# A post-norm transformer layer on one core: mask rows filled by two engines, a second store queue, TensorE occupied before the first exponential, feed-forward normalised in place

## What is computed

```python
q = einsum('btc,hcd->bhtd', x, Wq) + bq      # the same for k and v
scores = einsum('bhtd,bhsd->bhts', q, k) * D ** -0.5
probs = softmax(scores + causal, axis=-1)
x = layernorm(x + (einsum('bhts,bhsd->bhtd', probs, v) as [B, T, C]) @ Wo + bo)
gate = silu((x @ fp8(gate_w)) * gate_scale)
fuse = gate * ((x @ fp8(up_w)) * up_scale)
x = layernorm(x + (fuse @ fp8(down_w)) * down_scale)
```

## Time and profile before

| | us |
|---|---|
| median of 3 runs (lowest, highest) | 589.0 (588.6, 592.25) |
| the profiled execution's own time | 590.27 |
| its span, first to last instruction | 588.5 |
| TensorE busy | 539.8 (92%) |
| VectorE busy | 443.7 (75%) |
| ScalarE busy | 325.2 (55%) |
| GpSimd busy | 220.3 (37%) |

### The profile page before, as it was taken

How to read it: one execution, slowest core, us unless ns; L and a number is a source line. 1 busy time by engine, 2 the same in 40 slices (tenths; PEclk the granted TensorE clock), 3 DMA queues, 4 the chain that set the end, 5 groups by cost and what they waited for, 6 DMA issues and landing times.

```text
span 588.5 us, 10775 instructions
## 1 busy us (share of the span) xinstructions
PE 539.8 (92%) x3968; PEld 357.9 (61%) x3968; DVE 443.7 (75%) x802; ACT 325.2 (55%) x578; POOL 220.3 (37%) x250
## 2 busy tenths in 40 slices
PE   4568699999999999999999999987899999999993
PEld 1333356656566556665665656654378888888883
DVE  4476567788788878888878888878545877778765
ACT  1206456666766667667666576664854544345430
POOL 3004332433344333443254334421335553455442
PEclk9858989999999999999999999999999999999998
DMA  6878846547446564744654744520000001110012
GB/s 158 224 220 247 231 125 163 170 138 196 150 111 195 148 164 148 183 149 144 144 184 125 200 146 125 155 51 3 2 1 0 8 31 36 37 37 16 22 36 73
DMA packets 62959, 69.07 MB, mean 117 GB/s; under 512 B 7418, under 2 KB 57210, under 8 KB 62906
## 3 DMA queue, kind: packets, MB, share of 16 engines
q1 hardware_dynamic: 62074, 67.85, 40.2%
q10 hardware_dynamic: 832, 0.53, 0.3%
HBM read 37.63 MB, written 29.62 MB: 114 GB/s over the span
## 4 chain that ended last, share of the span: by engine, by line
PE 79%; DVE 6%; DMA 5%; issue 4%; ACT 3%; SPq 1%; POOL 1%; ACTq 0%; POOLq 0%; DVEq 0%
PE ps L1008 13%; PE ps L893 12%; PE ps L885 12%; PE ps L804 10%; PE ps L812 9%; PE ps L1021 7%; PE ps L869 7%; PE ps L870 4%; DVE nmax L576 2%; DMA q_st<-zero_rows 2%; PE ps L835 2%; PE ps L828 2%; DMA m_scratch<-mrow 2%; PE ps L846 1%; DVE hT_l L641 1%
## 5 line engine op out<-in xcount | busy, mean ns | idle before, releaser
L576 DVE TENSOR_REDUCE nmax<-ps 128x2 f32<-128x1024 f32 (+1 forms) x192 | 196.9, 1041 | 76.3 <-PE ps L870 76.1
L421 ACT ACTIVATE probs<-ps 128x512 f32<-128x512 f32 x320 | 183.3, 594 | 80.8 <-PE ps L885 80.7
L346 POOL TENSOR_SCALAR_AFFINE_SELECT probs<-probs 128x512 f32<-128x512 f32 x128 | 86.6, 690 | 199.4 <-ACT probs L421 199.4
L885 PE MATMUL ps<-q_st,k_st 98*128 98x384 bf16 (+3 forms) x512 | 123.3, 304 | 5.4 <-ACT probs L421 3.2
L869 PE MATMUL ps<-k_st,q_st 98*128 98x256 bf16 (+2 forms) x384 | 85.1, 282 | 14.9 <-DMA q_st<-zero_rows 10.8
L374 POOL TENSOR_TENSOR f_l<-f_full,f_h 128x512 fp32r<-128x512 f32 x48 | 61.6, 1290 | 76.6 <-ACT f_h L494 76.6
L870 PE MATMUL ps<-k_st,q_st 124*128 124x128 bf16 x512 | 86.8, 226 | 0.0
L893 PE MATMUL ps<-probs,v_st 128*32 128x512 f32 (+3 forms) x1024 | 84.1, 447 | 0.2
L885 PEld LDWEIGHTS ps<-q_st,k_st 98*128 98x128 bf16 x512 | 44.1, 98 | 50.7 <-issue 27.1
L489 ACT ACTIVATE sgate<-ps,s_gate 128x512 f32<-128x512 f32 x48 | 32.9, 688 | 63.0 <-PE ps L1008 63.0
L869 PEld LDWEIGHTS ps<-k_st,q_st 98*128 98x128 bf16 x384 | 38.5, 100 | 36.3 <-issue 14.7
(11 more groups left out here) (85 smaller groups left out, 810.5 us busy)
## 6 DMA issues: line engine op xcount, KB each, us to landing
q_st<-q_scratch SPq DMA_DIRECT2D x32, 384.0 KB
k_st<-k_scratch SPq DMA_DIRECT2D x32, 384.0 KB
q_scratch<-part SPq DMA_DIRECT2D x16, 384.0 KB, 3.6
k_scratch<-part SPq DMA_DIRECT2D x16, 384.0 KB, 2.8
xT<-in_attn_xT SPq DMA_DIRECT2D x8, 512.0 KB, 3.9
q_scratch<-part SPq DMA_DIRECT2D x16, 256.0 KB, 3.7
k_scratch<-part SPq DMA_DIRECT2D x16, 256.0 KB, 2.0
resid<-in_attn_x SPq DMA_DIRECT2D x8, 512.0 KB, 3.8
```

The source lines that it names most:

```text
L346: pool.affine_select(out=blocks, in_=blocks, compare_op=ALU.is_ge, fill=0.0, base=0, pattern=[*pattern, [1, P]], channel_multiplier=-1).th ...
L421: act.activation(probs[:, u, :], ps[:, u % 2, :], ACT.Exp, scale=SCALE).then_inc(exp_done, 1)
L576: dve.tensor_reduce(nmax[:, i, heads[0]:heads[-1] + 1], src, AX.X, ALU.max, negate=True).then_inc(max_taken, 1)
L885: m = pe.matmul(ps[:, u % 2, c0:c0 + T - P * j], k_st[0:RP, g, h, P * j:P * j + P], q_st[0:RP, g, h, P * j:T], start=True, stop=True)
```

## The change

- **Mask rows.** The two DMAs that copied the mask patterns are gone. `fill_mask` copies a pattern into the stacks of two groups in one instruction: VectorE for groups 0 and 1, GpSimd for groups 2 and 3, each for queries and keys. The patterns now lie on the partitions of their stack rows. The copies begin at partition `R0` = 96, so they also write stack rows 96 and 97, and `load_stack(0, 0)` waits for VectorE's copies and `load_stack(0, 2)` for GpSimd's.
- **Constants.** The memsets of `v_st` move behind the first parts, the one of `k_st`'s rows 0 and 1 is split between VectorE and GpSimd, and the zero rows of all groups come by one DMA at the start in place of one in each first `load_stack`.
- **Two store queues.** ScalarE issues the stores of the high and middle key parts of groups 0 and 1, and the store and load of the first group's maxima. SyncE issues the biases; `xT` of sequence 1 is loaded before the parts are stored.
- **TensorE occupied.** `keep_warm` issues matmuls on a tile of zeros: 10 before the projections, 4 behind the first V projection, 2 behind nearly each unit of maxima of groups 0 and 1. ScalarE's first activation runs on the same tile. `project_qk(0, 0)` waits for the query weights alone.
- **Feed-forward.** `norm_in` writes into `resid`; it stands before `fuse(n+1, 2)`. `make_hT(n + 2)` stands before `gate_up(n+1, 4)` and no longer behind it. The statistics of the output stand before `fuse(n+1, 4)` and the moments before `fuse(n+1, 5)`; `take_rstd2(n)` stands before `f_lo(n+1, 5)`.
- **Tail.** The last `down` goes by chunks into four banks, and the last output is stored in two halves.

The normalisation has moved ahead of the sums whose first halves (`y_sum<-ps`) release `make_hT`. The diff, cut to its core:

```diff
+        def fill_mask(eng, stack, rows, g):
+            return eng.tensor_copy(stack[R0:RA, g:g + 2].rearrange("p g h (b t) -> p (g h b) t", b=TB),
+                                   rows[R0:RA, :].unsqueeze(1).to_broadcast([RA - R0, 2 * HG * TB, P]))
...
@@ SyncE
+                if n:
+                    sp.dma_start(q_st[0:RM, g], zero_rows[:, :].unsqueeze(1).to_broadcast([RM, HG, T])).then_inc(stack_loaded[g], 16)
...
-            sp.wait_ge(pool_const, CONSTS)
-            for stack, rows in ((q_st, mask_q), (k_st, mask_k)):
-                sp.dma_start(stack[RP:RA].rearrange("p g h (b t) -> p (g h b) t", b=TB),
-                             rows[:, :].unsqueeze(1).to_broadcast([RA - RP, G * HG * TB, P])).then_inc(mask_loaded, 16)
+            load_xT(1)
             store_parts(0, 0)
-            store_parts(0, 1)
-            sp.wait_ge(dve_const, 6)
+            sp.wait_ge(lo_ready[1], 1)
+            sp.dma_start(k_scratch[0:P, 0:3, :], part[:, 1, :, :]).then_inc(part_stored[1], 16)
+            sp.wait_ge(mask_filled, 2)
             load_stack(0, 0)
             load_stack(0, 1)
             store_parts(0, 2)
             store_parts(0, 3)
+            sp.wait_ge(mask_filled_late, 3)
             load_stack(0, 2)
-            load_xT(1)
-            store_mrow(0, 0)
-            load_mrow(0, 0)
...
@@ GpSimd
+            pool.memset(k_st[0:RM, 2:G].rearrange("p g h t -> p (g h t)").bitcast(F32), ONES).then_inc(mask_filled_late, 1)
+            pool.wait_ge(pool_const, CONSTS)
+            for stack, rows in ((q_st, mask_q), (k_st, mask_k)):
+                fill_mask(pool, stack, rows, 2).then_inc(mask_filled_late, 1)
...
@@ ScalarE
+            for m in (0, 1):
+                hi_part(0, m, MX + m)
+            for m in (0, 1):
+                mid_part(0, m, probs[:, m, :])
+            dst = k_scratch[0:P]
+            act.wait_ge(mid_ready[1], 1)
+            act.dma_start(dst[:, 3:5, :], part[:, 1, 0:2, :]).then_inc(part_stored[1], 16)
+            act.dma_start(dst[:, 5:6, :], part[:, 1, 0:1, :]).then_inc(part_stored[1], 16)
...
             empty_mT(0)
+            act.wait_ge(mT_out, 1)
+            act.dma_start(m_scratch[0], mrow[0:RM * HG, :]).then_inc(mrow_stored[0], 16)
+            act.wait_ge(mrow_stored[0], 16)
+            act.dma_start(q_st[0:RM, 0], m_scratch[0].rearrange("(a h) t -> a h t", h=HG)).then_inc(mrow_loaded[0], 16)
...
@@ TensorE
+            def keep_warm(count):
+                for _ in range(count):
+                    pe.matmul(ps[:, 1, :], warm[:, 0:P], warm[:], start=True, stop=True)
...
+            pe.wait_ge(warm_ready, 1)
+            keep_warm(10)
...
             for u in range(NM):
                 scores_max(0, u)
+                if u:
+                    keep_warm(2)
             scores_max(1, 0)
             transpose_max(0)
             for u in range(1, NM):
                 scores_max(1, u)
+                keep_warm(2)
...
                 if nxt:
                     gate_up(n + 1, 1 - par, 3)
+                if nxt2:
+                    make_hT(n + 2)
+                if nxt:
                     gate_up(n + 1, 1 - par, 4)
-                if nxt2:
-                    make_hT(n + 2, par)
-                if nxt:
                     gate_up(n + 1, 1 - par, 5)
```

More of the change, by code:

```diff
@@ L385, in _ @@
             for n in range(B):
-                for ic in range(IC):
-                    if n + 1 < B:
+                if n + 1 < B:
+                    for ic in range(IC - 1):
                         f_lo(n + 1, 1 - n % 2, ic)
                 take_rstd2(n)
+                if n + 1 < B:
+                    f_lo(n + 1, 1 - n % 2, IC - 1)
         @block.scalar
@@ L499, in _ @@
                         empty_ynT(B - 1, 1, MB)
[L500 removed]
+                    if n > 0 and n + 1 < B and ic == 4:
                         for c in range(KC):
@@ L773, in _ @@
                 if nxt:
+                    out_stats(n, 0)
+                    out_stats(n, 1)
+                    fuse(n + 1, 4)
+                    out_moments(n)
                     fuse(n + 1, 5)
-                    out_stats(n, 0)
-                out_stats(n, 1)
-                out_moments(n)
-                if not nxt:
+                else:
+                    out_stats(n, 1)
+                    out_moments(n)
                     norm_out(n)
```

171 lines of the change are left out of this document (103 added, 68 removed).

## The result

| | before | after |
|---|---|---|
| median (lowest, highest), 16 runs each | 589.63 (588.07, 593.65) | 587.47 (586.83, 589.05) |
| span of the profiled execution | 588.5 | 585.1 |
| TensorE's mean granted clock | 0.967 | 0.971 |

The ratio of after to before is 0.9958, with an interval of 0.9942 to 0.9974. The change wins 0.0042 x 589.6 = 2.5 us where 8.3 were predicted, which is less than the 1% that the prediction took as the bound of no change. The interval leaves out 1, so a small gain is real.

A forecast was written before the change was run, and what follows sets the result against it. Bounds: the start's transfers and waits, one feed-forward wait a period, VectorE's tail; mid-attention is TensorE-bound. Terms 0.3 + 0.35 - 2.3 - 2.6 - 3.0 - 0.5 - 0.5 = -8.25 take 589.0 to 580.7 us; forecast within 578.5 to 583, full range 574.0 to 584.5.

The forecast's parts named there:

- the round trip of the maxima: Start, group 0's maxima through DRAM: on ScalarE's queue the trip fits under TensorE's own work, -2.3 us.
- the bound of 0: Round trip of the maxima: the gain is 0 instead of -2.3 us if the store still takes 4.77.
- TensorE's own order: Between transposes and first scores: group 1's maxima units and the last two occupying matmuls need 5.2 us.
- The first exponentials: Dense TensorE work from 42.8 on: 5.2 us at the low clock take half at the high level, -2.6 us.
- Rival 2: Waits only change name: slow round trip, low clock or down_out eats the gain; any one 583.0 to 583.7; chance 0.20.
- The start up to the first stack: From projections to first stack issue: early projections' gain is lost to the port GpSimd and VectorE share, +0.3 us.
- The maxima: Maxima loop of group 0: clock starts low and TensorE leads for three or four units, +0.35 us.
- From there to 73.8 nothing changes: First exponentials to 73.8 us: no change; the wait for the next stack, bound by DMA engines, moves along.
- Feed-forward: Feed-forward periods: earlier transposes remove the hT_l wait but slip 0.2; 0.5 us a period won, -3.0 in all.
- Tail: Last down by chunks: only 8 of 48 matmuls remain behind the last f_lo, now behind GpSimd's rstd; -0.5 us.
- the last store: End of the span: half the bytes in the last output store save about 0.5 of 3.4 us, -0.5.

The follow-up runs named there:

- e7_trip_port: After, with SyncE issuing the first round trip ahead of the bulk loads and GpSimd's memset and mask copies started behind the last low part; 578.4 us (0.9794).
- e14_all_late: After with SyncE's round trip before bulk, GpSimd copies behind low parts, wider act_warm, and up/down weights, output weights and scales loaded later; 568.2 us (0.9630).
- e1_hold_bulk: After, with SyncE waiting until the first group's maxima are back in the stack before issuing load_raw(0), load_x(0) and load_stack(0, 3); 583.4 us (0.9886).
- e3_no_port: After, with GpSimd starting its memset and mask copies only when VectorE has written all four low parts; 584.6 us (0.9901).
- e13_after_weights_late: After, with only the loads of the feed-forward up and down weights moved to the second sequence's turn; 581.3 us (0.9860).
- e6_aligned: After, with act_warm 48 bytes wider so that later SBUF tiles begin at a multiple of 64 bytes again; 585.4 us (0.9912).
- e5_ffn_alone: Before, with only the new feed-forward stage and tail, keeping its own start and SBUF layout; 583.4 us (0.9880).

## Why the prediction was wrong

**The failed step is the round trip of the maxima**: "On ScalarE's own queue I take 2.3, which makes 1.2 + 2.3 + 1.5 = 5.0 and lies under the 5.2." The sum for it was -2.3. Transposes to first scores took 44.60 - 33.76 = 10.84 us, 7.48 before, so the term is +3.4. It has two errors. The store was priced by its queue, from the 1.46 us of a later one that had nothing ahead of it; behind the 768 KB of the third stack it takes 4 to 5 us (e7_trip_port 4.02, e14_all_late 4.17, e2_sync_trip 4.95, all from SyncE), and from ScalarE, behind 2.4 MB, it took 5.37. And the bound of 0 was no bound: the prediction counted what the trip had ahead of it and not what the move released. SyncE's wait for the trip had held back 2 MB; with the wait gone they ran beside it, and the load, 1.48 us before, took 4.37. e1_hold_bulk, which only holds these transfers back, is 4.1 us quicker than after, and e2_sync_trip, which restores the old order on SyncE, 4.9. Even there the trip takes 7.50 us, as before, and e1_hold_bulk, with the trip on ScalarE's queue, is no quicker in total than this kernel. TensorE's own order, taken as 5.2, was 5.6 (7.50 less its wait of 1.91).

**The first exponentials, -2.6, fell with it.** The wait before them was to shrink from 1.75 us to nothing and grew to 5.27, and the clock was at the low level for some 5 of the 5.5 us from 44.60 on, as before. In e2_sync_trip the clock is 1.00 there. From the first scores to the fourth group's maxima it takes 22.59 us there, 24.97 in after and 25.40 before: the mechanism was right and its condition did not hold. Rival 2 ("the waits only change their name") named both effects, but with prices of +2.3 and +2.6, measured from the forecast; the first turned out at 5.7.

**The start up to the first stack** was +0.3 predicted and -1.05 measured, the size alone. The order was the worked one: the first `first_lo` waited for the first copy, the second for the second copy. But all of it came sooner. GpSimd's first copy started at 9.98 and not at 10.5; the copies took 3.59 and 4.06 us (3.9 taken), and the second started without the 0.7 us of `first_lo` between them, so the second `first_lo` ended at 18.12 and not at 19.7. The key store landed after 2.30 us (2.9), and VectorE's copy took 1.22 (1.5). The page weighed there, the Trainium skill, "GPSIMD Engine Reference", section "Performance versus the Vector engine", gives 3.5 by estimate; the copies of 3.59 us in after (the first) and of 3.60 in e3_no_port agree. Nothing was said of the other way out, to start GpSimd later, which is worth 2.9 us.

**The maxima**, +0.35 predicted, were -0.55 (26.17 to 33.76 is 7.59 us, 27.20 to 35.34 before 8.14). This is less than the scatter of the place in kernels with the same start. Behind the maxima the clock was 1.00 already, by the window from 34.00 of e2_sync_trip, whose work up to there is the same.

**"From there to 73.8 nothing changes"** was half right. The wait for the next stack did move along: after is 1.78 us behind before at the first scores, 1.35 and 1.22 at the fourth and the fifth group, on either side of the wait, and 0.77 at the first `gate_up`. What gave back the last 0.45 was not looked into. But the prediction took this wait for a fixed one. It hid 7 us, more than twice any term of the sum (e13_after_weights_late), and anything won ahead of it is partly lost there (2.7 us of the 5.7 in e2_sync_trip).

**Feed-forward**, -3.0 predicted: six periods shorter by 0.55 are -3.3, the stage in all -2.9. VectorE's order came out as worked out (releasing half of the sum at 510.48 + 0.68, 7.0 behind the start of `down`, for 7.75), and the transposes followed `gate_up` without a gap at 511.66. The sum missed the layout, which costs 1.4 to 1.8. **Tail**, -0.5: -0.55, and **the last store**, -0.5: -0.7.

## What to carry to other kernels

When a wait is taken off a queue, list what stood behind it and price that beside the thing you wanted to hasten: here 2 MB overtook an 8 KB round trip. Look for the wait that gives gains back before adding more gains ahead of it; stalls of 2.46 and 4.36 us each cost some 2.8 us more here, because TensorE's clock fell behind them, and loads that are first read a hundred microseconds later have no place ahead of it. A small helper tile can move all later tiles in SBUF, so compare the spacing of matmuls that the edit doesn't touch.

## What the runs showed of the hardware

- A transfer of 8 KB behind 768 KB took 4.0 to 5.0 us to be answered (e7_trip_port 4.02, e2_sync_trip 4.95), and 5.37 behind 2.4 MB (after). The 8 KB of the way back took 1.45 us with nothing beside them and 4.37 with 2 MB.
- VectorE's two instructions with two inputs in SBUF, 0.7 us each by themselves, waited for one of GpSimd's copies each and ended 0.54 us behind its end (14.11 behind 13.57, 18.12 behind 17.58), though the copies ran without a gap. The second copy took 4.06 us, 0.47 more than the first.
- The time of the same matmuls differed by 2 to 5% with the place of the tiles in SBUF: 40 of `gate_up` in 9.41, 9.25 or 9.18 us, 48 of `down` in 5.68, 5.45 or 5.75 (after, e6_aligned, e5_ffn_alone; `down` in e6_aligned took 5.45 in four of seven periods and 5.66 in three). The layout that is best for one was not best for the other.
